# Four written-out turn strings replaced: the order in which each engine serves four independent batch elements

## The reference

```python
# layer 0: decayed linear attention; feed-forward with 8 experts, the two best per token
# layer 1: 4 blocks of causal linear attention (16 heads of 8), each with LayerNorm, 128->512->128 with gelu,
#          LayerNorm; then 8 experts, two per token
# layer 2: gated delta rule over chunks (triangular solve, then a recurrence over chunks); one expert per sequence
# layer 3: gated delta rule with a learned decay per token and an output gate; one expert per sequence
```

## Time and profile before

| what | us |
|---|---|
| median of 3 runs | 1829.18 (1828.34 to 1829.65) |
| the profiled execution, its own time | 1830.12 |
| its span, first to last instruction | 1828.3 |
| PE busy | 1759.1 (96%) |
| DVE busy | 1274.2 (70%) |
| POOL busy | 1177.2 (64%) |
| ACT busy | 1082.8 (59%) |
| mean granted PE clock | 0.996 |

### The profile page before, as it was taken

The page is one execution under the profiler, slowest core; times in us unless marked ns, Lnnn a source line. Parts: engine busy times, 40 slices in busy tenths (PEclk is TensorE's granted clock), DMA queues, the critical chain, the costliest instruction groups (busy, mean ns, idle before and its releaser), DMA issues.

```text
span 1828.3 us, 31828 instructions
## 1 busy us (share of the span) xinstructions
PE 1759.1 (96%) x10270; PEld 1338.7 (73%) x10270; DVE 1274.2 (70%) x4547; ACT 1082.8 (59%) x2686; POOL 1177.2 (64%) x1547
## 2 busy tenths in 40 slices
PE   7999999999999999999999999999998999999988
PEld 5788988866676666666666676677878887788874
DVE  7863345688869887888889765546557766678684
ACT  5554226566676577777676775456545556544555
POOL 5555658888878877878778863134437664454456
PEclk9999999999999999999999999999999999999999
DMA  6100000010000000000000000000000000000002
GB/s 241 65 25 1 1 3 2 3 48 1 1 2 1 1 1 1 1 1 1 1 1 1 6 5 5 1 1 8 3 1 3 11 21 17 20 2 1 2 9 62
DMA packets 24473, 26.44 MB, mean 14 GB/s; under 512 B 3492, under 2 KB 21284, under 8 KB 23924
## 3 DMA queue, kind: packets, MB, share of 16 engines
q1 hardware_dynamic: 24308, 24.41, 4.1%
HBM read 22.26 MB, written 2.15 MB: 13 GB/s over the span
## 4 chain that ended last, share of the span: by engine, by line
PE 79%; DVE 8%; POOL 6%; ACT 4%; issue 2%; DMA 1%; SPq 0%; POOLq 0%; DVEq 0%; ACTq 0%
PE ps L86 72%; PE ps L89 7%; POOL arena L103 5%; ACT arena L97 4%; DVE arena L103 3%; DVE arena L143 1%; DVE arena L106 1%; DVE arena L109 1%; DVE arena L126 1%; ACT L97 0%; DMA cst<-in_cst 0%; DVE arena L123 0%; DVE arena L129 0%; DVE arena L112 0%; DVE ps L143 0%
## 5 line engine op out<-in xcount | busy, mean ns | idle before, releaser
L103 POOL TENSOR_TENSOR arena<-arena 128x128 f32<-128x128 f32 (+6 forms) x796 | 693.5, 885 | 348.0 <-DVE arena L103 127.5
L97 ACT ACTIVATE arena<-ps 128x128 f32<-128x128 f32 (+13 forms) x1100 | 352.8, 354 | 435.2 <-PE ps L86 312.6
L86 PE MATMUL ps<-arena 128*128 128x128 f32 (+4 forms) x2864 | 460.3, 295 | 18.6 <-DVE arena L103 11.5
L86 PEld LDWEIGHTS ps<-arena 128*128 128x128 f32 x2864 | 381.4, 192 | 118.3 <-issue 63.1
L103 DVE TENSOR_TENSOR arena<-ps,arena 128x128 f32<-128x128 f32 (+4 forms) x696 | 319.1, 470 | 179.4 <-PE ps L86 162.8
L97 ACT ACTIVATE arena<-arena 128x128 f32<-128x128 f32 (+1 forms) x772 | 299.8, 442 | 35.3 <-POOL arena L103 27.5
L97 ACT ACTIVATE arena<-ps,cols 128x512 f32<-128x512 f32 x324 | 218.3, 689 | 170.9 <-PE ps L86 156.0
L86 PE MATMUL ps<-arena,cst 128*128 128x504 f32 (+2 forms) x768 | 289.2, 493 | 8.2 <-POOL arena L103 3.1
L86 PE MATMUL ps<-arena,moe 128*128 128x256 f32 (+1 forms) x960 | 289.7, 441 | 0.6 <-DVE arena L103 0.6
L89 PE MATMUL ps<-cst,arena 128*128 128x128 f32 (+1 forms) x1392 | 238.4, 275 | 14.8 <-ACT arena L97 6.3
L109 DVE SCALAR_TENSOR_TENSOR arena<-ps,arena 128x128 f32<-128x128 f32 (+2 forms) x424 | 141.9, 373 | 131.0 <-PE ps L86 87.1
(11 more groups left out here) (110 smaller groups left out, 1847.6 us busy)
## 6 DMA issues: line engine op xcount, KB each, us to landing
rows<-in_rows SPq DMA_DIRECT2D x1, 2253.0 KB, 15.1
arena<-in_x SPq DMA_DIRECT2D x8, 256.0 KB, 5.0
wf<-in_wf SPq DMA_DIRECT2D x2, 1024.0 KB, 5.9
arena<-in_L_ffn_W SPq DMA_DIRECT2D x8, 256.0 KB, 3.2
out_dram<-arena SPq DMA_DIRECT2D x8, 256.0 KB, 2.8
wmod<-in_wmod SPq DMA_DIRECT2D x4, 384.0 KB, 7.7
arena<-kept SPq DMA_DIRECT2D x24, 64.0 KB, 2.8
arena<-kept SPq DMA_DIRECT2D x8, 192.0 KB, 3.1
```

The costliest lines, as they stand in the source:

```text
L86: return UNSENT if self.e is None else self.e.matmul(out, lhsT, rhs, start=start, stop=stop)
L97: return self.e.activation(out, in_, func, bias=bias, scale=scale)
L103: return UNSENT if self.e is None else self.e.tensor_tensor(out, a, c, op)
```

## The change

All four strings of `TURNS` are replaced by others, almost from their first digit on. Each engine's string now has two more digits per part, which are calls to generators that have already ended and issue nothing. The set of instructions is the same on PE, DVE, POOL and SP; on ACT one `ACT_TABLE_LOAD` less is in the stream (92 for 93). Nothing else of the file is touched.

```diff
 TURNS = {
-    "pe": ("0123440000000000200022000122200012210001110021101322000111300031133300013332001113332222221133311122"
...
+    "pe": ("0120000300000020002200012220001101112200021310012001103120003310113032033301322123324211133132112122"
...
```

More of the change, by code:

```diff
@@ new lines @@
+    "act": ("4442300140000202122212111103003313334211224030000333000010112010000020212030130020110022032220302211"
+           "0031012322123102210113221231101212033011021120033112311113113222112311213132200030000111120312003330"
+           "0023011320002310030110200033030230001112002012202100323322001031332111310220000010212211120012003000"
+           "2322212001331123123322120320000310211131332233102320200333310113230121112020223111113311023332022202"
+           "3113333230000001313131133200231022232202130031333031110203310003333110233212222000130022333222331102"
+           "2311211120330233310001211211312232201332110130001123200021322112332113331020022000010112213213312333"
+           "0322122111121010000302322233331100111101022303311022330322002223011131112033023130120222002101132233"
+           "3133031010100003122232213323003100320321102211020001001121300211100012230332111010112000202012221233"
+           "1101302130000230222333111230201331332012302222300330201222112111120003301203111122201133023312303301"
+           "2022222132113311013322002320221002111133332210311312222210302333313000011111033333310322222301321333"
+           "3223002011110133002030023303321222211310000230110320200002222012033030123202100011330232213222210021"
+           "2111310233232233123111211010000221122223211110031100021233332232102321113110332211113002221232201020"
+           "0231300003013300322211100011100331102011033301200121113002010221000222023200320332113332300302303113"
+           "2223300211133231223311123333301132331212311333222223211220310331231201100002033323002033220133122303"
+           "0111103321310332030311312031330023332220321233020322033003302103320120132000112000131122132110202333"
+           "3023310112213301320212302302100311120311003220112200313223003310302212331023312300103002311123102011"
+           "3321332211300123221033310023121200311131123223210013330110302200332231102113301303322220230112201332"
+           "1310122331110333033310332333021120012000223231223013301332210300131122003113310232302110312000231120"
+           "0230122213133300322301320212231111032123010233122223102121201230133003320023132030213321230130111031"
+           "1230112320312222002132333121301333210023311324223302230102200300311131110311122022221000112131033113"
+           "33222133330000022332132221333223233413002"),
```

152 lines of the change are left out of this document (81 added, 71 removed).

## The result

| | before | after |
|---|---|---|
| median | 1829.41 (1828.34 to 1829.73, 4 runs) | 1783.71 (1783.02 to 1784.88, 4 runs) |
| ratio of the times | | 0.9752 (95%: 0.9735 to 0.9769) |
| profiled execution, own time | 1830.12 | 1784.88 |

What follows compares the result with a forecast made beforehand. PE was taken to bound the kernel (busy 1759.1 of 1828.3 us), so only its waits could move. Start 2.0, layer 1's blocks 1.85 + 6.0 and clock 1.8 make 11.7 us less: 1817.5 us, range 1803 to 1831.

Steps and rivals of the forecast that it cites:

- What bounds it, and where: PE bounds the kernel; its idle time is largest in layer 1's blocks, expected to fall from 24.6 to about 17 us.
- Layer 1's blocks, 6.0 + 1.85 us: 366 to 1098 us: 32 fewer short covers save 6.0 us (0 to 14.7), one removed wait for ACT saves 1.85.
- short covers: Waiting places with under 384 columns of PE products since the product they depend on; 53 to 21 in layer 1's blocks.
- slower: Rival, above 1832.8 us, chance 0.13: layer 1's blocks get 88 more waits on paths through several other-engine instructions; 1837 us.
- The 1.85 us of the earlier trace: PE's wait for ACT at 1024.24 us goes because element 2's copy now precedes eight normalizations: 1.85 us less.
- Start, 2.0 us: Up to 91 us: more cover at two PE waits for DVE, 2.0 us less (0 to 3.5).
- Clock, 1.8 us for 1020 to 1040: Granted clock of 0.91 in this stretch becomes full once the wait there goes: 1.8 us less (0 to 7.0).
- the clock variant of the larger gain: All low-clock stretches go with the waits: 16.9 us less, 1812 us; no chance of its own.
- larger gain: Rival, below 1809 us, chance 0.17: nearly all 32 places waited, plus start, ACT wait and clock; 22 to 27 us less.
- Shared port, 0: DVE and POOL blocking each other costs DVE 6 us, hidden by its slack, so costed at 0.
- From 1281 us on, 0 with 4 to either side: From 1281 us to the end: counts of covers are level, so no gain, 4 us either way.
- Waits only move: Rival, 1825.5 to 1832.8 us, chance 0.17: each closed wait opens one of its size, so the terms cancel; 1829.

Runs made afterwards that it cites:

- only_dve: Kernel before with only DVE's string new in layer 1's blocks, other engines' strings old, 189 of 3842 DVE turns held back against deadlock: 2007.7 us, ratio 1.0972.
- two_places: Kernel before, PE's string old; DVE's common share and neighbouring turns moved earlier in the start, one ACT copy put ahead of eight normalizations: 1830.5 us, ratio 1.0003.
- n_early: Kernel before with the new order only up to the start of layer 1's blocks: 1825.7 us, ratio 0.9978.
- n_late: Kernel before with the new order only behind layer 1's blocks (its experts, layers 2 and 3): 1819.3 us, ratio 0.9945.
- n_l1: Kernel before with the new order in layer 1's blocks only: 1805.9 us, ratio 0.9870.

## Why the prediction was wrong in size

- **What bounds it, and where**: right. PE's work is the same to 0.1 us, layer 1's blocks are the largest place, and the waits there fell to 25 (forecast under 40), none above 1.5 us. PE idle fell further than forecast, to 9.3 instead of 17 us.
- **Layer 1's blocks, 6.0 + 1.85 us**: the failing step, 28.7 measured. Three sizes in it were wrong. First, the price was PE's *idle* time. The stage had 24.6 us idle but 55.4 us loss; the gain is 15.3 of idle and 13.4 of busy time. I had written that idle time understates, and then used it as it stood. Second, the share of 0.44 of short covers that wait was a ratio of unlike things. Of the 53 places 38 really waited, of the 21 left 15 do: 23 waits gone at short covers, not 14, and 6.8 us. Third, and largest, covers from 512 columns on were costed at nothing and gave 15.3 us at waits, 24.6 less 9.3, with 93 and 79 waits. At the same count of columns the other side was less late. The upper bound of 14.7 for this term rested on the same idle time and on short covers alone, so the range could not hold it.
- **The long paths** of the rival "slower": 88 more, as counted. The waits on them rose only from 38 to 45, and their loss fell from 13.1 to 7.2 us. Length of a path was not lateness, in an order whose strings fit. In only_dve it was: the mechanism exists, the count does not tell when it acts.
- **The 1.85 us of the earlier trace rows**: the wait is gone, but its price as a single place is nothing (two_places).
- **Start, 2.0 us**: 4.1 measured (n_early 4.4), above my upper end of 3.5; and not by the share moved on DVE, with which alone the start takes 86.2 us for 85.8.
- **Clock, 1.8 us for 1020 to 1040**: not borne out. n_late has that stretch in the old order without the dip, and its blocks take 731.9 us against 732.0. Its row:

```profile
1015.00:1035.00 20.00, 16.63 (x77) 10.29 (x77) 14.62 (x60) 11.83 (x28) 19.04 (x20) 1.00 0.00 0
```

Elsewhere it may count: before, the last stretch has 0.92 and 0.73 between 1770 and 1790, two_places 0.83 over the same 20 us, n_late 1.00 there. By 0.17 x 20 up to 3.4 of the 6 us in the last stretch may be clock; that wasn't tried by itself. The low stretches of the earlier trace rows make 7.0 us; while PE works the changed kernel has one, 0.83 from 110 to 120 us, which is 1.7. So the clock is worth at most 5.3 us in all, and the clock variant of the larger gain is a small part of it. The text's own test, "if PE's busy time itself changes by more than 7 us, the clock or hidden waits decided", came true by hidden waits.
- **Shared port, 0**: not nothing. I took 345 ns, the mean of the form that reads PSUM, as undisturbed; the form that reads SBUF takes 282 ns in the mean where no POOL operation runs beside it (61 of the 224) and 406 where one does, so POOL beside it cost DVE some 20 us before and not 6. In layer 1 the zero held. From 1281 us on up to 6 us hang on it.
- **From 1281 us on, 0 with 4 to either side**: 12.2 measured, with level counts; PE's idle time there fell from 30 to 21 us. Here the count of covers was blind. The one table load less wasn't tried by itself.
- **The rivals**: "larger gain" had the right mechanism and was capped at 27 us by the idle time. "Waits only move" is what happened to two_places. Against it stood only the count, and for the whole kernel the count was right about the sign alone.
- **Beyond the count's reach**: in layer 1's blocks n_l1 and only_dve differ by 3.0, 2.1 and 1.2 places a turn in the mean in PE's, ACT's and POOL's strings (and by 0.4 in DVE's), and by 202 us. Their short covers differ by 71, which at the prediction's 0.19 us each would be 13.

## What to carry to other kernels

Price a late engine by the start-to-start intervals of the one that bounds, not by its idle time: in layer 1's blocks before, the loss was over twice the idle time (55.4 and 24.6 us). An interleaving written out for several engines is one object. Change the strings together and cut them where all of them can be cut. Treat a wait seen at one place as a symptom: in two_places, the operation taken out of its way only moved it. A count of distances in one engine's stream gave the sign here; the size would have needed the other engines' durations along the path. What made the other side less late at long covers in the new order wasn't isolated.

## What the runs showed of the hardware

- **Dips of the granted clock come and go under the same instruction order.** From 110 to 120 us the kernel before had 0.83 with 58 matmuls; two_places, with the same order there, 1.00 and 72, and that stage takes 273.4 instead of 275.0 us. PE was busy for 9.81 us of the ten in both, so no idle time in the records explains it; what does stays open. The row of two_places, against the first of the earlier trace rows:

```profile
110.00:120.00 10.00, 9.81 (x72) 8.74 (x71) 9.31 (x65) 7.86 (x19) 8.30 (x13) 1.00 0.10 27
```

- **DVE's scaling with an accumulator output** is slower alone (337 and 82 ns for the read, against a median of 282) and yet the old order became 2.5 us faster with it (1827.3 for 1829.9). Its duration no longer varied with POOL's work (longest 347 ns); that this is the reason was not tried apart.
- **From the end of another engine's operation to the start of the product that waits for it** PE needs 52 to 54 ns at best, before and after. Where a separate semaphore instruction stands ahead of the weight load as well, the waits gather at 143 to 147 ns: in the kernel before, all 66 places of that kind that lost over 0.05 us have one, against 21 of 142 of the first kind.
